# Routing, one-hot tiles and weight loads of a mixture-of-experts layer, on one core

## The chip, the cores and the metric

One core of a Trainium2 chip. The metric is the device time of one execution in microseconds (us).

## The reference, cut to what matters

```python
x = x + _L0_xattn_ref(_layernorm(x), ctx, ...)      # 16 query heads, 8 key/value heads
x = x + _L0_ffn_ref(_layernorm(x), ...)             # the part that the change touches
...                                                 # three more pairs of attention and feed-forward
def _L0_ffn_ref(x, router_logits, gating_einsum, linear, per_expert_scale, router_scale):
    ...
    probs = jax.nn.softmax(logits32, axis=-1)
    _, choices = jax.lax.approx_max_k(logits32, k=k)                # 2 of 8 experts
    ...
    sorted_xs = x_flat[xs_indices, :]                               # 4096 rows, sorted by expert
    gate_out = jax.lax.ragged_dot(sorted_xs, w_gate, group_sizes=tokens_per_expert)
    activation = jax.nn.gelu(gate_out[:, 0, :]) * gate_out[:, 1, :]
    expert_outputs = jax.lax.ragged_dot(activation, linear, group_sizes=tokens_per_expert)
    expert_outputs = expert_outputs * per_expert_scale[expert_indices, None]
    out = jnp.einsum('blkd,blk->bld', out, combine_weights)
```

There are 2048 tokens of 512 values. Every token goes to two of eight experts. Each expert has an up matrix of 512 x 1024 and a down matrix of 512 x 512.

## The kernel before, in words

The program is written by hand for each engine, and the engines meet on semaphores only. TensorE is called PE, VectorE DVE, ScalarE ACT, GpSimd POOL and SyncE SP. Layer 0's attention is the "wide" stage. `wide_steps` (line 449) yields one list of steps, and every engine goes through the same list and does its part of each step. So the order in that list is the order of the work on every engine. The expert stage follows, and its list is `block_steps` (line 1235). Between the stages stands `fence` (line 215): each of the five engines drains, adds one to a semaphore and waits until all five have done so.

The end of the wide stage forms the last rows of the layer. `late_norm` (line 386) normalises a tile of 128 rows, SP stores it to DRAM (`sp_late`, line 400), `late_ln` turns it on PE and ACT copies the high part out, and `late_low` (line 434) makes the low part on DVE. `logits` k (line 1467) multiplies 512 tokens by the router, `route` k (line 1485) turns these logits so that tokens lie on partitions, and `best` (line 1608) finds the best experts on DVE. The wide stage does routes 0 to 2 and two of the three best steps. Route 3 (first line of `pe_experts`, line 1495) and the last best step (in `dve_experts`, line 1622) lie behind the fence.

Behind the fence POOL makes small constants (line 1398 on), among them a triangle and a row of counting numbers. PE counts the tokens of each expert with matmuls, and DVE works out each token's place. A place p is block p // 128 and position p % 128. OB is a one-hot tile of the block, OS one of the position: 32 operations of 128 x 128 elements. POOL and ACT scale OB into ON, and PE multiplies OS and ON into a table that says which token stands at each place. POOL gathers the rows of a block by this table with an indirect DMA (line 1442), three blocks ahead, and scatters the results (line 1447). DVE also writes EI, three values for each of the 39 blocks: the expert, whether it differs from the one before, and which half of the weight buffers it uses. `known` tells the others that EI is there.

For a block j PE does `turn` (the gathered rows), `upper` (24 matmuls with the up weights in WU), `mid` (turns the hidden rows), `lower` (12 matmuls with the down weights in WD). Upper j + 1 is done before lower j. At blocks 3, 5, 24 and 28 a projection for the next layer is added, and at block 10 a small step. WU and WD have two halves each. SP issues `wup` and `wdown` of every block in the order of the list. It reads three registers from EI, and the issue is conditional: if the expert is the same as in the block before, nothing is moved, though the semaphore still counts. `wup` j waits until block j - 2 has used its weights, and `wdown` j until block j - 2 has used its down weights:

```python
                row = bass.ds(ex * 128, 128)
                if step == "wup":
                    sp.wait_ge(S["up"], 2 * (j - 1))
                    sp.e.dma_start(w["WU"][:, bass.ds(bu * 8192, 8192)].bitcast(F32), self.MW[row, 0:8192], cond=ch
                                   ).then_inc(S[f"moeu{j % 2}"], 16)
```

An up load is 4 MB (128 x 8192 values of 4 bytes), a down load 2 MB. In the queue of SP also stand `dca` (constants and copies for the next layer, at blocks 1, 9 and 32) and `narrow` (its weights, at block 12).

Of the kernel before, what the change touches and what calls it, by code (L numbers as in the profile page):

```python
# [17 lines left out]
NBLK = 39  # L18
# [14 lines left out]
    "ones": 1, "anym": 2, "mrow": 3, "onesb": 4, "erl": 5, "erlo": 6, "evar": 7, "oa": 8, "edl": 9, "first": 10, "eplace": 11, "eob": 12, "eoh": 13, "eone": 17, "tokens": 18, "known": 19, "eow": 20, "vdd": 21, "vzero": 22, "gqk": 23, "crl": 24, "cwl": 25, "cprob": 27, "ccc": 28,  # L33

    "ers": 1, "iota": 2, "tri": 5, "places": 7, "esel": 11, "eon1": 12, "egate": 14, "eg3": 19, "ready1": 20, "ready2": 21, "mfl": 22,
# [19 lines left out]
           "moeu0": 320, "moeu1": 304, "ht": 39, "hh_turned": 39, "up": 78, "xst": 39, "xs_turned": 39}  # L55
# [106 lines left out]
class Program:  # L162
    def __init__(self, nc, ins, out):
# [21 lines left out]
        self.rs = self.sb("rs", [128, NT], F32)  # L185
        self.st = self.sb("st", [128, NT, 6], F32)
# [262 lines left out]
    def wide_steps(self, L):  # L449
# [101 lines left out]
        if l0:  # L551
            yield "route", 2
            yield "best", 0
            yield "best", 1
# [228 lines left out]
    def sp_wide(self, sp, L):  # L783
# [4 lines left out]
        for step, g in self.wide_steps(L):  # L788
# [321 lines left out]
    def dve_wide(self, dve, L, steps=None):  # L1110
# [9 lines left out]
        for step, u in steps or self.wide_steps(L):  # L1120
# [107 lines left out]
            if step == "best":  # L1228
                self.dve_route_best(dve, u)
# [49 lines left out]
    def expert_tiles(self):  # L1279
# [26 lines left out]

        mu = self.place[0]["mu8"]
# [5 lines left out]
        stand(base + 65536, mu)  # L1313
        sb("ON", [128, 2 * NT, 2, 40], BF16)
        sb("OA", [128, NT, 8], BF16)
        sb("tri", [128, 128], BF16)
        sb("all1", [128, 128], BF16)
        sb("e8", [128, 5, 8], F32)
        sb("n8", [128, 2, 8], I32)
        sb("zero", [128, 8], F32)  # L1320
        sb("pb", [128, 2 * NT], BF16)
        stand(mu + 2048, base + 90112)
        sb("OB", [128, 2 * NT, 40], BF16)
        sb("OG", [128, 2 * NT, 3, 40], BF16)
        sb("esc", [128, 8], F32)
        sb("oh", [128, 2, NT, 8], F32)
        sb("pos", [128, NT, 8], F32)
        sb("i8f", [128, 8], F32)
        sb("jio", [128, 40], F32)
        sb("jr", [128, 40], F32)  # L1330
        sb("pf", [128, 2, NT], F32)
        sb("pi", [128, 3, 2 * NT], I32)
        sb("pl", [128, 2 * NT], F32)
        sb("g3", [128, 3, 2 * NT], BF16)
        sb("ga", [128, 2, NT], F32)
        sb("es", [128, 2, NT], F32)
        sb("number", [128, 40], F32)
        sb("tf", [1, 1], F32)

        w["OS"] = self.at("eOS", [128, 2 * NT, 128], BF16, self.xl_at + 16384)  # L1340
        stand(base + 32768, base + 65536)
# [5 lines left out]
        sb("pc", [128, 1], F32)  # L1347
        sb("trf", [128, 128], F32)
        sb("tm", [128, 2, NT, 8], F32)
        sb("te", [128, 2, NT, 8], F32)  # L1350
        sb("ge", [1, 40, 8], F32)
# [12 lines left out]
    def sp_experts(self, sp):  # L1364
# [30 lines left out]
    def pool_experts(self, pool):  # L1395
        S, w = self.S, self.W["e"]
        P1, at = S["pool_one"], ONE["esel"]
        pool.e.iota(w["i8f"][:], [[1, 8]], base=0, channel_multiplier=0, allow_small_or_imprecise_dtypes=True)
        pool.e.iota(w["jio"][:], [[1, 40]], base=0, channel_multiplier=0, allow_small_or_imprecise_dtypes=True).then_inc(P1, 1)
        pool.e.memset(w["trf"][:], 1.0).then_inc(P1, 1)  # L1400
        pool.wait_ge(P1, ONE["tri"] - 2)
        pool.e.affine_select(out=w["trf"][:], in_=w["trf"][:], compare_op=ALU.is_gt, fill=0.0, base=0,
                             pattern=[[1, 128]], channel_multiplier=-1).then_inc(P1, 1)
        pool.e.memset(w["all1"][:], 1.0)
        pool.wait_ge(P1, ONE["tri"] - 1)
        pool.copy(w["tri"][:], w["trf"][:]).then_inc(P1, 1)
        pool.e.iota(w["jr"][:], [[128, 40]], base=0, channel_multiplier=0, allow_small_or_imprecise_dtypes=True)
        pool.e.iota(w["io"][:], [[1, 128]], base=0, channel_multiplier=0, allow_small_or_imprecise_dtypes=True)
        pool.e.iota(w["ic"][:], [[1, 2 * NT]], base=0, channel_multiplier=0, allow_small_or_imprecise_dtypes=True)
# [2567 lines left out]
```

## Time and profile before

| what | value |
|---|---|
| median of 3 runs | 3536.63 us |
| lowest and highest run | 3533.78 and 3544.22 us |
| the profiled execution | 3552.24 us |
| its span, first to last instruction | 3550.5 us |
| PE busy, share of the span | 93% |
| DVE, ACT, POOL busy | 67%, 44%, 35% |
| mean granted clock of TensorE | 0.970 |

The profile is one execution. Busy shares are averages over stages that are bound by different things. The wide stage of layer 0 ends at about 794 us, the expert blocks run from about 820 to 1215 us, and two thirds of the kernel lie behind them.

### The profile page before, as it was taken

What the parts mean: (1) busy time and instruction counts of PE and PEld (TensorE: products, weight loads), DVE (VectorE), ACT (ScalarE), POOL (GpSimd) and SP (SyncE); (2) the same over time, 40 slices, a digit from 0 to 9 for tenths busy, and PEclk for the clock granted to TensorE, in tenths of its full rate; (3) what the DMA queues carried; (4) which work ended last, traced back from release to release, by engine and by line L of the source; (5) the groups of instructions that cost most, each with busy time, mean ns of one, the idle gap of its engine ahead of it and who ended that gap; (6) DMA issues with size and microseconds to landing.
All of it is one profiled execution on the core that took longest, in us unless ns stands there. A gap on an engine that the chain in (4) does not pass through costs nothing.

```text
span 3550.5 us, 60357 instructions
## 1 busy us (share of the span) xinstructions
PE 3291.5 (93%) x22499; PEld 2711.5 (76%) x22499; DVE 2377.9 (67%) x4731; ACT 1572.4 (44%) x3398; POOL 1238.5 (35%) x1169
## 2 busy tenths in 40 slices
PE   7999999997999879998999979998889999999987
PEld 6899899875777646655899855554679999999976
DVE  6677778784323368876644458776677777777786
ACT  5766666541111145553222224444245555555551
POOL 1023333342243277762322236555621111111232
PEclk9999999997999989999999999999999999999999
DMA  3356666215655210001111046563011111111101
GB/s 140 99 194 230 225 229 203 79 56 201 223 205 198 73 36 26 23 6 50 48 37 54 22 121 168 142 164 90 31 48 48 60 59 55 48 60 48 61 25 51
DMA packets 186248, 349.35 MB, mean 98 GB/s; under 512 B 20168, under 2 KB 91976, under 8 KB 181096
## 3 DMA queue, kind: packets, MB, share of 16 engines
q1 hardware_dynamic: 179720, 325.04, 28.6%
q0 software_dynamic: 6240, 20.45, 1.6%
q8 instruction: 183, 3.00, 0.4%
q14 instruction: 105, 0.86, 0.1%
HBM read 436.26 MB, written 101.97 MB: 152 GB/s over the span
## 4 chain that ended last, share of the span: by engine, by line
PE 18%; issue 14%; DVE 10%; POOL 5%; ACT 2%; DMA 2%; SPq 1%; DVEq 0%; POOLq 0%; ACTq 0%
PE banks L109 17%; POOL kst L92 2%; DMA nqT<-head_stacks 1%; POOL qst L92 1%; PE banks L222 1%; DVE K L92 1%; ACT P L83 1%; DVE qst L103 1%; SPq L106 1%; POOL nPS L92 1%; DVE P L96 1%; POOL kvl L92 1%; DVE X L92 1%; DVE st L278 1%; DVE nmx L103 1%
## 5 line engine op out<-in xcount | busy, mean ns | idle before, releaser
L92 DVE TENSOR_TENSOR X<-X,banks 128x512 f32<-128x512 f32 x352 | 238.8, 680 | 129.0 <-PE banks L109 128.7
L103 DVE TENSOR_REDUCE nmx<-banks 128x4 f32<-128x1024 f32 (+2 forms) x256 | 238.6, 953 | 122.1 <-PE banks L109 121.1
L92 POOL TENSOR_TENSOR slo<-sraw,shi 128x512 fp32r<-128x512 f32 x108 | 141.7, 1312 | 362.7 <-ACT shi L86 359.8
L83 ACT ACTIVATE nPT<-banks 128x1024 f32<-128x1024 f32 x192 | 196.2, 1023 | 143.9 <-PE banks L109 141.7
L92 POOL TENSOR_TENSOR kst<-kst,mhalf 128x4 f32<-128x4 f32 x64 | 64.6, 1010 | 558.5 <-DVE kst L97 558.5
L109 PE MATMUL banks<-XH,tT 128*128 128x256 f32 x1024 | 245.7, 284 | 7.7 <-DVE XL L92 4.5
L109 PE MATMUL banks<-XL,tT 128*128 128x256 f32 x1024 | 244.3, 283 | 0.0
L109 PE MATMUL banks<-WU,exh 128*128 (+1 forms) x624 | 209.7, 408 | 15.9 <-DMA WU<-expert_parts 14.4
L109 PE MATMUL banks<-woh,OH 128*128 128x512 f32 x512 | 214.4, 419 | 8.3 <-DVE X L92 5.4
L83 ACT ACTIVATE P<-banks,nb,qst 128x256 f32<-128x256 f32 x256 | 141.1, 561 | 180.9 <-DVE nb L92 180.9
L109 PEld LDWEIGHTS banks<-XH,tT 128*128 128x128 f32 x1024 | 197.0, 192 | 10.9 <-DVE XL L92 6.1
L109 PE MATMUL banks<-woh,OL 128*128 128x512 f32 x512 | 202.7, 396 | 0.0
L109 PE MATMUL banks<-wol,OH 128*128 128x512 f32 x512 | 202.3, 395 | 0.0
L92 POOL TENSOR_TENSOR nPS<-nPT 128x512 f32<-128x512 f32 x128 | 162.7, 1276 | 108.4 <-PE banks L109 95.8
L109 PEld LDWEIGHTS banks<-XL,tT 128*128 128x128 f32 x1024 | 196.7, 192 | 0.8
L109 PE MATMUL banks<-kvh,CX 128*128 128x256 f32 x1024 | 190.0, 283 | 0.0
L92 POOL TENSOR_TENSOR rs<-sc,mhalf 128x1 f32<-128x1 f32 x128 | 81.7, 642 | 269.7 <-DVE sc L96 269.6
L103 DVE TENSOR_REDUCE mx<-banks 128x2 f32<-128x512 f32 x256 | 174.6, 682 | 1.8 <-PE banks L109 1.5
L92 DVE TENSOR_TENSOR PL<-banks,PH 128x512 fp32r<-128x512 f32 x256 | 164.0, 681 | 14.3 <-ACT PH L86 14.1
L92 POOL TENSOR_TENSOR tHL<-thf,tHH 128x512 fp32r<-128x512 f32 x64 | 82.6, 1291 | 253.5 <-ACT tHH L86 253.5
L83 ACT ACTIVATE P<-banks,nb 128x256 f32<-128x256 f32 x256 | 117.8, 472 | 116.6 <-DVE nb L96 116.3
L96 DVE TENSOR_SCALAR P<-P,rc 128x256 f32<-128x256 f32 x512 | 164.0, 383 | 4.6
(468 smaller groups left out, 10508.9 us busy)
## 6 DMA issues: line engine op xcount, KB each, us to landing
WU<-expert_parts SPq DMA_DIRECT2D x39, 4096.0 KB
WD<-expert_parts SPq DMA_DIRECT2D x39, 2048.0 KB
CX<-context_parts SPq DMA_DIRECT2D x64, 512.0 KB, 3.3
sraw<-in_moe_w SPq DMA_DIRECT2D x96, 256.0 KB, 3.3
expert_parts<-shi SPq DMA_DIRECT2D x96, 256.0 KB
expert_parts<-slo SPq DMA_DIRECT2D x96, 256.0 KB
head_stacks<-nTK SPq DMA_DIRECT2D x48, 256.0 KB
head_stacks<-nTQ SPq DMA_DIRECT2D x48, 256.0 KB, 3.7
```

Of the source, the lines that this page charges most:

```text
L83: return self.e.activation(out, in_, func, **kw)
L92: return self.e.tensor_tensor(out, a, b, op)
L96: return self.e.tensor_scalar(out, a, s1, None, op0)
L103: return self.e.tensor_reduce(out, a, AX.X, op, **kw)
L106: return self.e.dma_start(out, in_)
L109: return self.e.matmul(out, l, r, start=start, stop=stop, skip_group_check=skip)
L222: return pe.e.transpose(out, in_, self.ident[0:n, 0:n])
L278: dve.e.bn_stats(self.st[:, t, :], self.X[:, t, :]).then_inc(S["bn"], 1)
```

## The change

The changes of order are in the two lists. Route 3 and all the finding of the best experts no longer stand behind the fence: `fence` is split into `leave` and `enter`; PE, DVE and POOL leave where they left before and enter later. POOL's constants are made in a new step `ones` of the wide stage. OS is made by two operations of 16 x 128 elements. Expert 0's up weights are loaded by SP in step `late_norm` 13, and the load of block 0 is now conditional on the first expert in use being another. SP waits, for its loads, on a value that it reads from a new table EW: for block j, twice (up) or once (down) the index of the last block before j at which the expert changed, and at least 1. The waits on `ewt` (the gates product) before the up loads are gone. The tiles of the routing lie at other addresses.

```diff
@@ def fence
+    def leave(self, e):
+        e.e.drain().then_inc(self.S["fence"], 1)
+    def enter(self, e, k):
+        e.wait_ge(self.S["fence"], 5 * k)
     def fence(self, e, k):
-        e.e.drain().then_inc(self.S["fence"], 1)
-        e.wait_ge(self.S["fence"], 5 * k)
+        self.leave(e)
+        self.enter(e, k)
@@ def wide_steps
         yield "late_low", 11
-        for t in (14, 15):
-            yield "late_ln", t
         if l0:
+            yield "ones", 0
             yield "route", 0
+        yield "late_ln", 14
+        if l0:
             yield "route", 1
+        yield "late_ln", 15
         for t in (12, 13, 14, 15):
             yield "late_low", t
...
         if l0:
             yield "route", 2
-            yield "best", 0
-            yield "best", 1
@@ def sp_wide
                 self.sp_late(sp, g)
+            if l0 and step == "late_norm" and g == 13:
+                sp.wait_ge(S["y"], 128)
+                sp.dma(self.W["e"]["WU"][:, 0:8192].bitcast(F32), self.MW[0:128, 0:8192]).then_inc(S["moeu0"], 16)
@@ def pool_wide
+            if step == "ones":
+                self.pool_route_ones(pool)
@@ def dve_wide
-            if step == "best":
-                self.dve_route_best(dve, u)
@@ def block_steps
-        for j in range(3):
-            yield "wup", j
-            if j < 2:
-                yield "wdown", j
+        yield "wup", 0
+        yield "wdown", 0
+        yield "wup", 1
+        yield "wup", 2
+        yield "wdown", 1
@@ def sp_experts
                     bu, ch = 0, None
+                    if step == "wup":
+                        ch = sp.e.value_load(w["one"][0:1, 1:2], min_val=0, max_val=1)
+                        sp.wait_ge(S["moeu0"], 16)
                 else:
                     sp.wait_ge(S["dve_one"], ONE["known"])
-                    sp.wait_ge(S["pe_one"], ONE["ewt"])
+                    if step == "wdown":
+                        sp.wait_ge(S["pe_one"], ONE["ewt"])
...
                 if step == "wup":
-                    sp.wait_ge(S["up"], 2 * (j - 1))
+                    if j > 1:
+                        free = sp.e.value_load(w["EW"][0:1, 0, j:j + 1], min_val=1, max_val=2 * NBLK)
+                        sp.wait_ge(S[f"moeu{j % 2}"], 16 * (j // 2 + 1 - j % 2))
+                        sp.e.wait_ge(S["up"], free)
...
                 else:
-                    sp.wait_ge(S["down"], j - 1)
+                    if j > 1:
+                        free = sp.e.value_load(w["EW"][0:1, 1, j:j + 1], min_val=1, max_val=NBLK)
+                        sp.wait_ge(S[f"x{j % 2}"], 16 * (j // 2 + 1))
+                        sp.e.wait_ge(S["down"], free)
@@ def pool_experts (the constants moved, unchanged, to pool_route_ones, behind sp "ov" 64)
+        self.enter(pool, 1)
         pool.wait_ge(S["dve_one"], ONE["tokens"])
@@ def pe_experts
         for i in range(2 * NT):
-            pe.wait_ge(S["dve_one"], ONE["eoh"] + i // 8)
+            pe.wait_ge(S["dve_one"], ONE["eoh"] + i // NT)
...
+        self.enter(pe, 1)
         for step, j in self.block_steps():
...
-                pe.wait_ge(S[f"moeu{j % 2}"], 16 * (j // 2 + 1))
+                pe.wait_ge(S[f"moeu{j % 2}"], 16 * (j // 2 + 2 - j % 2))
@@ def dve_experts
-        self.dve_route_best(dve, 2)
         dve.e.memset(w["zero"][:], 0.0)
+        for k in range(3):
+            self.dve_route_best(dve, k)
...
+        dve.ts(w["one"][0:1, 1:2], w["tf"][0:1, 0:1], 1.0, None, ALU.min)
         dve.copy(w["one"][0:1, 0:1], w["tf"][0:1, 0:1]).then_inc(S["dve_one"], 1)
...
-        dve.copy(pb[:], pi[:, 2, :]).then_inc(S["dve_one"], 1)
-        dve.wait_ge(S["rt"], a)
-        c = rt(dve.copy(w["pl"][:], pi[:, 1, :]))
+        dve.copy(pb[:], pi[:, 1:3, :]).then_inc(S["dve_one"], 1)
         dve.wait_ge(S["dve_one"], ONE["eplace"])
+        dve.wait_ge(S["fence"], 5)
...
-        for i in range(2 * NT):
-            m = dve.ts(w["OS"][:, i, :], w["iob"][:], w["pl"][:, i:i + 1], None, ALU.is_equal)
-            if i % 8 == 7:
-                m.then_inc(S["dve_one"], 1)
+        for k in range(2):
+            place = pb[:, 0, NT * k:NT * k + NT].unsqueeze(2).to_broadcast([128, NT, 128])
+            dve.tt(w["OS"][:, NT * k:NT * k + NT, :], w["iob"][:].unsqueeze(1).to_broadcast([128, NT, 128]), place, ALU.is_equal
+                   ).then_inc(S["dve_one"], 1)
...
         rt(dve.copy(EI[:, 2, :], r0(2)))
+        b = rt(dve.tt(r0(3), r0(1), w["jio"][0:1, :], ALU.mult))
+        dve.wait_ge(S["rt"], b)
+        b = rt(dve.e.tensor_tensor_scan(r0(4), r0(3), r0(7), 0.0, ALU.max, ALU.add))
+        dve.wait_ge(S["rt"], b)
+        for k in range(2):
+            rt(dve.ts(w["EW"][:, k, 1:40], r0(4)[:, 0:39], 2.0 - k, 1.0, ALU.mult, ALU.max))
@@ def pe_program, dve_program, pool_program
-        self.fence(pe, 1)
+        self.leave(pe)
...
```

## Rows read from the trace of the kernel before

**Rows 1.** Waits of PE, 820 to 1216 us: us in total, times, longest

```profile
PE banks L109 <- DMA WU<-expert_parts: 14.4, 8, 3.6
```

**Rows 2.** Timeline of PE, turning hidden rows: start, us, engine, line, operation

```profile
832.85 0.60 PE L222 MATMUL banks<-ident,eh 128*128 128x128 f32 x4
...
843.71 0.60 PE L222 MATMUL banks<-ident,eh 128*128 128x128 f32 x4
...
1066.83 0.60 PE L222 MATMUL banks<-ident,eh 128*128 128x128 f32 x4
...
1075.98 0.60 PE L222 MATMUL banks<-ident,eh 128*128 128x128 f32 x4
...
1086.85 0.60 PE L222 MATMUL banks<-ident,eh 128*128 128x128 f32 x4
...
1200.49 0.60 PE L222 MATMUL banks<-ident,eh 128*128 128x128 f32 x4
```

**Rows 3.** Timeline of PE, first up matmul of blocks 5 and 13 [idle before]

```profile
876.39 0.79 PE L109 MATMUL banks<-WU,exh 128*128 x1 [2.89 <-DMA WU<-expert_parts]
...
959.71 0.50 PE L109 MATMUL banks<-WU,exh 128*128 x1 [1.01 <-DMA WU<-expert_parts]
```

**Rows 4.** Timeline of SP's issues, 834 to 947 us

```profile
834.70 0.11 SPq L1383 DMA_DIRECT2D WU<-expert_parts  x1
836.86 0.09 SPq L1387 DMA_DIRECT2D WD<-expert_parts  x1
...
859.87 0.37 SPq L1383 DMA_DIRECT2D WU<-expert_parts  x1
...
946.15 0.36 SPq L1383 DMA_DIRECT2D WU<-expert_parts  x1
```

**Rows 5.** Timeline of PE, 782 to 822 us

```profile
782.78 0.66 PE L222 MATMUL banks<-ident,late 128*128 128x128 f32 x4 [1.00 <-DVE XL L92]
...
784.42 1.95 PE L109 MATMUL banks<-e,elgT 16*128 16x8 f32 x16
...
794.13 1.87 PE L109 MATMUL banks<-e,elgT 16*128 16x8 f32 x8 [1.42 <-DVEq L217]
...
811.65 0.71 PE L109 MATMUL banks<-eON,eOS 128*128 128x80 bf16 x8 [0.59 <-DVE eOS L96]
820.13 1.12 PE L222 MATMUL banks<-ident,exs 128*128 128x128 f32 x4 [7.77 <-DMA exs<-rows_in,etok]
```

**Rows 6.** Timeline of DVE, 796 to 812 us

```profile
796.11 0.19 DVE L89 COPY eLG<-banks 128x32 f32<-128x32 f32 x1 [2.08 <-PE banks L109]
...
797.23 0.16 DVE L1620 FIND_INDEX8 ei<-em,eLG 128x8 uint32<-128x8 f32 x1
...
802.77 1.49 DVE L92 TENSOR_TENSOR eOB<-ejb,epb 128x1280 bf16<-128x1280 bf16 x1
804.18 7.41 DVE L96 TENSOR_SCALAR eOS<-eiob,epl 128x128 bf16<-128x128 bf16 x32
```

**Rows 7.** Timeline of POOL, 804 to 815 us

```profile
804.34 2.33 POOL L92 TENSOR_TENSOR eON<-eOB,eicb 128x1280 bf16<-128x1280 bf16 x1 [3.75 <-DVE eOB L92]
...
813.58 1.28 POOL L1442 DMA_INDIRECT exs<-rows_in,etok  x1 [0.86 <-DVE etok L1715]
```

**Rows 8.** Instructions on tile eOS: duration ns min/median/max, first and last start

```profile
L96 DVE TENSOR_SCALAR eOS<-eiob,epl x32: 240/241/2374, 804.2 to 811.4; 128x128 bf16<-128x128 bf16 x32
```

**Rows 9.** Timeline of all engines, 637 to 643 us, POOL and DVE

```profile
637.77 1.21 DVE L92 TENSOR_TENSOR wql<-wqr,wqh 128x1024 fp32r<-128x1024 f32 x1
...
638.19 4.15 POOL L92 TENSOR_TENSOR slo<-slo,sraw 128x512 f32<-128x512 f32 x2 [1.63 <-DMA sraw<-in_L_ffn_factors]
...
638.90 2.32 DVE L92 TENSOR_TENSOR wol<-wor,woh 128x1024 fp32r<-128x1024 f32 x1
```

**Rows 10.** Line L1442, the gather issued at 813.58, and the one at 821.53

```profile
DMA to landing us min/median/max: 6.5/6.5/6.5
...
DMA to landing us min/median/max: 3.3/3.3/3.3
```

More of the change, by code:

```diff
@@ L31 @@
     "elt": 4, "etot": 5, "ecount": 6, "etab": 7, "ewt": 8, "vdp": 9, "tsum": 10, "clt": 11, "cgate": 12,
-    "ones": 1, "anym": 2, "mrow": 3, "onesb": 4, "erl": 5, "erlo": 6, "evar": 7, "oa": 8, "edl": 9, "first": 10, "eplace": 11, "eob": 12, "eoh": 13, "eone": 17, "tokens": 18, "known": 19, "eow": 20, "vdd": 21, "vzero": 22, "gqk": 23, "crl": 24, "cwl": 25, "cprob": 27, "ccc": 28,
-    "ers": 1, "iota": 2, "tri": 5, "places": 7, "esel": 11, "eon1": 12, "egate": 14, "eg3": 19, "ready1": 20, "ready2": 21, "mfl": 22,
+    "ones": 1, "anym": 2, "mrow": 3, "onesb": 4, "erl": 5, "erlo": 6, "evar": 7, "oa": 8, "edl": 9, "first": 10, "eplace": 11, "eob": 12, "eoh": 13, "eone": 15, "tokens": 16, "known": 17, "eow": 18, "vdd": 19, "vzero": 20, "gqk": 21, "crl": 22, "cwl": 23, "cprob": 25, "ccc": 26,
+    "iota": 1, "tri": 4, "places": 6, "ers": 7, "esel": 11, "eon1": 12, "egate": 14, "eg3": 19, "ready1": 20, "ready2": 21, "mfl": 22,
     "mask": 16, "rl_in": 48, "n_wd": 64, "n_pos": 80, "mbias": 96, "gqk_in": 128, "cw": 144,
@@ L185, in __init__ @@
         self.rs = self.sb("rs", [128, NT], F32)
+        self.st_at = self.top
         self.st = self.sb("st", [128, NT, 6], F32)
@@ L1305, in expert_tiles @@
         w["end"] = place[0]
+        w["EW"] = self.at("eEW", [1, 2, 40], I32, self.st_at)
         mu = self.place[0]["mu8"]
@@ L1311, in expert_tiles @@
         sb("i8", [128, NT, 8], U32)
-        stand(base + 65536, mu)
-        sb("ON", [128, 2 * NT, 2, 40], BF16)
+        sb("zero", [128, 8], F32)
+        stand(base + 65536 + 2048, mu)
+        sb("oh", [128, 2, NT, 8], F32)
         sb("OA", [128, NT, 8], BF16)
-        sb("tri", [128, 128], BF16)
-        sb("all1", [128, 128], BF16)
+        sb("pos", [128, NT, 8], F32)
+        sb("tm", [128, 2, NT, 8], F32)
         sb("e8", [128, 5, 8], F32)
         sb("n8", [128, 2, 8], I32)
-        sb("zero", [128, 8], F32)
-        sb("pb", [128, 2 * NT], BF16)
+        sb("pb", [128, 2, 2 * NT], BF16)
+        sb("pf", [128, 2, NT], F32)
+        sb("pi", [128, 3, 2 * NT], I32)
+        sb("tf", [1, 1], F32)
         stand(mu + 2048, base + 90112)
         sb("OB", [128, 2 * NT, 40], BF16)
+        sb("ON", [128, 2 * NT, 2, 40], BF16)
         sb("OG", [128, 2 * NT, 3, 40], BF16)
         sb("esc", [128, 8], F32)
[L1326 to L1336, printed above, removed]
         sb("number", [128, 40], F32)
-        sb("tf", [1, 1], F32)
         w["OS"] = self.at("eOS", [128, 2 * NT, 128], BF16, self.xl_at + 16384)
-        stand(base + 32768, base + 65536)
+        stand(self.place[0]["QH"], self.place[0]["P"])
         sb("io", [128, 128], F32)
@@ L1347, in expert_tiles @@
         sb("pc", [128, 1], F32)
+        sb("i8f", [128, 8], F32)
+        sb("jio", [128, 40], F32)
+        sb("jr", [128, 40], F32)
         sb("trf", [128, 128], F32)
-        sb("tm", [128, 2, NT, 8], F32)
+        sb("tri", [128, 128], BF16)
+        sb("all1", [128, 128], BF16)
         sb("te", [128, 2, NT, 8], F32)
+        sb("es", [128, 2, NT], F32)
+        sb("ga", [128, 2, NT], F32)
+        sb("g3", [128, 3, 2 * NT], BF16)
         sb("ge", [1, 40, 8], F32)
@@ L1397, in pool_experts @@
         P1, at = S["pool_one"], ONE["esel"]
[L1398 to L1409, printed above, removed]
-        pool.e.iota(w["pc"][:], [[1, 1]], base=1, channel_multiplier=1, allow_small_or_imprecise_dtypes=True).then_inc(P1, 1)
-        pool.wait_ge(P1, ONE["places"] - 1)
-        pool.copy(w["iob"][:], w["io"][:])
-        pool.copy(w["jb"][:], w["jio"][:])
-        pool.copy(w["icb"][:], w["ic"][:]).then_inc(P1, 1)
         te, es, ga, sm = w["te"], w["es"], w["ga"], w["sm"]
@@ L1454, in pool_experts, with pool_route_ones @@
                 self.pool_key_rows(pool, *j[:2])
+    def pool_route_ones(self, pool):
+        S, w, P1 = self.S, self.W["e"], self.S["pool_one"]
+        pool.wait_ge(S["ov"], 64)
+        pool.e.iota(w["i8f"][:], [[1, 8]], base=0, channel_multiplier=0, allow_small_or_imprecise_dtypes=True)
+        pool.e.iota(w["jio"][:], [[1, 40]], base=0, channel_multiplier=0, allow_small_or_imprecise_dtypes=True).then_inc(P1, 1)
+        pool.e.memset(w["trf"][:], 1.0).then_inc(P1, 1)
+        pool.wait_ge(P1, ONE["tri"] - 2)
+        pool.e.affine_select(out=w["trf"][:], in_=w["trf"][:], compare_op=ALU.is_gt, fill=0.0, base=0,
+                             pattern=[[1, 128]], channel_multiplier=-1).then_inc(P1, 1)
+        pool.e.memset(w["all1"][:], 1.0)
+        pool.wait_ge(P1, ONE["tri"] - 1)
+        pool.copy(w["tri"][:], w["trf"][:]).then_inc(P1, 1)
+        pool.e.iota(w["jr"][:], [[128, 40]], base=0, channel_multiplier=0, allow_small_or_imprecise_dtypes=True)
+        pool.e.iota(w["io"][:], [[1, 128]], base=0, channel_multiplier=0, allow_small_or_imprecise_dtypes=True)
+        pool.e.iota(w["ic"][:], [[1, 2 * NT]], base=0, channel_multiplier=0, allow_small_or_imprecise_dtypes=True)
+        pool.e.iota(w["pc"][:], [[1, 1]], base=1, channel_multiplier=1, allow_small_or_imprecise_dtypes=True).then_inc(P1, 1)
+        pool.wait_ge(P1, ONE["places"] - 1)
+        pool.copy(w["iob"][:], w["io"][:])
+        pool.copy(w["jb"][:], w["jio"][:])
+        pool.copy(w["icb"][:], w["ic"][:]).then_inc(P1, 1)
     def pool_gate_parts(self, pool):
@@ L1680, in dve_experts @@
         dve.wait_ge(S["rt"], a)
[L1681 to L1683 removed]
+        rt(dve.e.tensor_scalar(pi[:, 1, :], pi[:, 0, :], 127, None, ALU.bitwise_and))
+        a = rt(dve.e.tensor_scalar(pi[:, 2, :], pi[:, 0, :], 7, None, ALU.arith_shift_right))
+        dve.wait_ge(S["rt"], a)
         dve.wait_ge(S["pool_one"], ONE["places"])
[L1685 to L1687 removed]
+        dve.copy(pb[:], pi[:, 1:3, :]).then_inc(S["dve_one"], 1)
         dve.wait_ge(S["dve_one"], ONE["eplace"])
+        dve.wait_ge(S["fence"], 5)
         for i in range(2):
@@ L3839, in dve_program @@
         self.dve_wide(dve, 0)
-        self.fence(dve, 1)
+        self.leave(dve)
         self.dve_experts(dve)
@@ L3862, in pool_program @@
         self.pool_wide(pool, 0)
-        self.fence(pool, 1)
+        self.leave(pool)
         self.pool_experts(pool)
```

8 lines of the change are left out of this document (2 added, 6 removed).

## Prediction

> **What bounds the kernel now.** The change touches one stretch: the routing of layer 0 and the 39 expert blocks behind it. I read the waits of TensorE (PE) there first. Its largest entry is PE waiting for expert up weights, 14.4 us in 8 waits [rows 1]. A wait is not a price, so next comes the pace of the blocks in PE's timeline, by the four transposes of the hidden rows that each block has once. Two neighbours without any event are 9.15 us apart; with one extra key or value projection between them 10.87, so that costs 1.72; from block 0 to block 37 it is 367.64 us [rows 2]. 37 plain intervals are 338.6, the four projections 6.9, a small extra step at block 10 0.2. So 22.0 us are lost to the eight waits: more than the 14.4 idle, because matmuls behind a long stall run slow: 0.79 us for the first behind 2.89 us of idle, 0.50 behind 1.01 [rows 3]. One wait is at block 1. The interval before it ends (832.85 to 843.71) is 10.86, so 1.7 is lost there [rows 2]. The other seven, at the first block of each new expert (5, 9, 13, 18, 23, 28, 31), share 20.2.
>
> Why they come is in SyncE's (SP's) queue. An issue that moves data takes 0.35 to 0.38 us there, a skipped one 0.08 to 0.11. The load for block 5 goes out at 859.87 and PE starts on it at 876.39, 16.5 us later; the quickest, for block 13, takes 13.6 (946.15 to 959.71) [rows 3, 4]. SP may issue only when block j-2 has used its weights, about a block and a half ahead of need; that is shorter than the load.
>
> Ahead of the blocks nothing overlaps. PE's third quarter of routing is followed by 1.42 us for the barrier and 1.87 for the fourth [rows 5]; DVE finds the best experts from 796.11, builds OB at 802.77 and 32 one-hot tiles from 804.18 in 7.41 us [rows 6]; PE's last eight matmuls on them take 0.71 [rows 5]; POOL issues the first gather at 813.58 [rows 7], and PE turns its rows at 820.13 after 7.77 idle [rows 5]. This is one chain, and every us on it is a us of the kernel.
>
> **The change, part by part.**
>
> *Order and barrier.* PE idles 1.00 us before the turn of row tile 14, the two early routes behind it take 1.95 for 16 matmuls, 0.98 each [rows 5]. Route 0 now lies in the idle time, route 1 before turn 15, which logits 3 alone needs. Logits 2 starts at 782.78 + 0.6 (turn) + 0.98 + 0.6 = 784.95 instead of 786.3: 1.35 us. Route 2 then ends near 791.4 in place of 792.7, and route 3 follows without the 1.42. DVE no longer leaves the barrier between quarters: its 1.3 us for quarter 2 (the length of the same work from 796.11 to 797.3 [rows 6]) end at 792.7, when the fourth can begin, not at 796.11. That is 3.4. An added minimum and the place of the wider cast cost 0.1 each, the zero fill of 0.07 leaves the chain: **3.2 us**. Bounds: if the slower matmuls return (1.87 for route 3) and the 1.35 is lost, 1.5; if the logits matmuls behind them, about half of which ran slow, keep their pace too, 4.7 (an estimate). POOL's constants move into a stretch in which it only waits for DVE; their first reader comes some 10 us later, so they cost nothing, and 10 us late they would cost what they cost now.
>
> *Two operations for the one-hot tiles.* Before, 32 operations of 0.24 us that overlap, one of which took 2.37 [rows 8]: POOL's ON (804.34, 2.33 us [rows 7]) ran just then. Elsewhere two DVE operations with two SBUF inputs show the same exclusion both ways: POOL's subtraction of 638.19 starts when wql ends, and wol then takes 2.32 in place of 1.21 [rows 9]. The new operations have the operand form of OB, one side repeated and one broadcast: 1.49 us for 1280 elements [rows 6]; wql has 1.21 for 1024 [rows 9]. That is 1.1 ns an element, so 2048 take 2.3. The first starts at the end of OB, POOL's ON waits behind it, takes 2.3, and the second follows; less two overlaps of 0.1 that is 6.7 us in place of 7.4, of which the last operation's own overlap gives 0.1 back. PE's tail is now 16 matmuls, 1.4 us in place of 0.71. Net **0.1 us** less. Bounds: without exclusion 2.2 less; if POOL has to wait for both, all 32 matmuls come behind, 1.4 more. On this the Trainium skill, VectorE: DVE Perf Modes, section "The perf-mode tier table", has 1224 ns for a two-tensor operation of 2048 bf16 elements. By it each operation would be 1.1 us shorter and this part would bring 2.2. The row for 1280 elements has no such rate, and the sum goes by the row.
>
> *Expert 0's up weights early.* SP issues 4 MB behind row tile 13's store, at about 779.5, once the last output product is done. By the slowest block load (16.5) they are in at 796. SP then waits for them, skips the normal load (if the first expert is 0; with eight experts in use it is), and loads the 2 MB of down weights at about 800.5. Before, the first gather was issued while 6 MB were moving and needed 6.5 us; a later one in a quiet stretch 3.3 [rows 10]. Its first issue is 0.3 us longer than later ones, so 3.6: **2.9 us**. Bounds 0 and 3.2. Row tiles 14 and 15 are stored behind the 4 MB; OB waits for them at 799.6, which is 3 us later than the load's latest end.
>
> *Block 1.* SP no longer waits for the gates product before wup 1 and issues it some 12 us ahead of need: **1.7 us**, bounds 0 and 1.7.
>
> *Register waits.* DVE computes them in four operations, 0.7 us, behind the tokens that POOL needs: they delay only `known`, which PE wants 14 us later. On SP a step is 2.16 us (834.70 to 836.86 [rows 4]); a fourth register adds about a third of three reads, 0.6, so 2.8 a step, 5.5 a block, under 9.15. Behind the waiting SP instruction are the skipped loads, the constants of the next stage and the next real load. The register holds the start of the previous expert, so wup(c) may go when its buffer is free, but wup(c+1) waits until block c-1 is through upper, and wdown(c+1) until block c-1 is through lower. For the next change c2 = c+4 the load is therefore issued at least 3 steps (8.1 us) behind the lower step of c-1 and needed three blocks and a turn, 27.8 us, behind it: 19.7 us ahead against 13.6 to 16.5. For c+3 (28 to 31) 15.9 plus the projection's 1.7; for 9 to 13 another 3.8 us of SP's copies lie between: 15.9. The narrowest is block 5: the floor of 1 holds wdown 2 until block 0's down product is done, just before block 1's transposes (843.71 [rows 2], less the 7.9 us won by then: 835.8). Then wup 4, wdown 3, seven constant loads (an estimate: 0.5 each, from the 0.35 of a plain issue) and wup 5 follow, 847.7. It is needed at 876.39 - 2.89 - 7.9 = 865.6 [rows 3], 17.9 later. All seven losses go: **20.2 us**. Bounds 14 (block 5 keeps its 5.9) and 20.2. What is late next is nothing on PE: blocks at 9.15.
>
> **Sum**: 3.2 + 0.1 + 2.9 + 1.7 + 20.2 = 28.1 us. The profiled execution has 3552.24 us (span 3550.5), so it would be 3524.1; it lies 15.6 above the median of the runs, and nothing in the sum scales with that, so 3536.63 - 28.1 = **3508.5 us**.
>
> **Rivals.**
> *First boundary stays.* SP's steps are longer than 2.8, or wup 5 goes with the constants just issued and takes over 17.9 us. Block 5 keeps up to 5.9: 3514.4. For: the 16.5 of this very load. Chance 0.2.
> *The routing gain is given back.* The late row tiles land behind the 4 MB (on each DMA engine descriptors are taken in ring order: the Trainium skill, DMA: Bandwidth & Descriptors, "Queues, rings and completion order"; no row here shows it), or the slow level comes back: the 3.2 go and OB waits some us more. 3511.7 to 3514. Chance 0.15.
> *The stalls change their place.* Loads of 6 MB beside gathers and scatters (a gather needs up to 6.5 beside them [rows 10]) or some other queue hold PE at the boundaries; half of the 20.2 and the gather's 2.9 stay: 3521.5. If all 20.2 stay, the change does not do what it says: 3528.7. Chance 0.12.
> *Slower.* SP becomes the pace. If a register read or a wait on a register costs far more than the reads in this trace, a step passes 4.6 us and two of them the block's 9.15. At 5.4 us a step 37 blocks lose 1.65 each, 61 us, against 28: 3569. It decides from 4.6 on and outweighs the gain from about 5.0. Against it: 2.16 with three reads [rows 4]. Chance 0.03.
>
> **How the numbers follow.** The forecast has 0.5. Its own range by the bounds: 3505 to 3513. Eight in ten with the first two rivals, half of the third and some us of run to run spread: 3502 to 3522. A measurement of this kernel tells about 0.3% (10.6 us) from no change. Faster by more needs 3526 or less: all but the last tenth, 0.93; within it 0.04; slower 0.03.
>
> **What would show it.** In the profile of after: transposes of block 0 and 37 about 345.7 us apart (338.6 + 7.1); no wait for WU at changes of expert, real up loads 20 to 45 us ahead of use; first gather landing in under 4 us; the fourth quarter's best experts from about 792.7; OS in two operations near 2.3 us, one of them near 4.4 with POOL's ON inside. Wrong would be: a wait for WU at block 5, SP steps over 4.6 us, OB waiting for a DMA, or a distance from block 0 to 37 that stays over 360.

## The result, and the profile of the changed kernel

The changed kernel takes 3519.5 us (median of 6 runs, 3518.7 to 3526.61) against 3544.33 for the kernel before on the same chip (6 runs, 3533.78 to 3551.73): ratio 0.9938, 95% interval [0.9918, 0.9958], or 22 us less by the ratio, between 15 and 29; the two medians lie 24.8 apart. The forecast was 28.1 less and 3508.5 us, 3505 to 3513 by the bounds of its terms and 3502 to 3522 with rivals and spread. The direction holds, and so does the wider range; the time lies outside the narrower one, and the gain was forecast too large. Of the 11.0 us between 3508.5 and 3519.5, 7.7 are in the base: three more runs moved the median of before from 3536.63 to 3544.33. The profiled execution of the changed kernel has 3518.88 us (span 3517.1), against the 3524.1 that the prediction gave for it from the profile of before.

The two profiles, set side by side by stages, with those of three more executions from later runs of the same two kernels (each stage is the distance between the first starts of the events named, in us; the ends are good to 0.1):

| stage | before | before, 2nd | after | after, 2nd | after, 3rd |
|---|---|---|---|---|---|
| start to store of row tile 13 | 778.9 | 782.3 | 778.9 | 783.0 | 783.4 |
| to the cast of the best experts | 18.51 | 16.12 | 13.30 | 14.86 | 13.28 |
| to the turn of block 0 | 22.72 | 22.57 | 20.37 | 20.76 | 20.57 |
| to block 0's hidden rows | 12.71 | 12.57 | 11.75 | 12.98 | 13.13 |
| block 0 to block 37 | 367.64 | 365.77 | 347.12 | 347.14 | 347.15 |
| from there to the end | 2349.9 | 2344.7 | 2345.7 | 2340.2 | 2347.3 |

Two stages that the change does not touch, the first and the last, differ by up to 4.5 and 9.7 us between executions. The first pair of profiles is therefore 33.4 us apart although the kernels differ by 22.

First the waits of PE in after from 820 to 1184 us, which is the expert stretch. These are all that come to over 1 us, where before had 14.4 us for WU [rows 1]:

```profile
PE banks L109 <- DVE ehl L92: 2.2, 1, 2.2
PE banks L109 <- issue: 1.2, 1, 1.2
```

PE's timeline of after, for [rows 5] and the ends of [rows 2] (start, us, engine, line, operation, idle before):

```profile
781.70 1.05 PE L109 MATMUL banks<-e,elgT 16*128 16x8 f32 x8
782.77 0.66 PE L231 MATMUL banks<-ident,late 128*128 128x128 f32 x4
783.36 1.05 PE L109 MATMUL banks<-e,elgT 16*128 16x8 f32 x8
784.35 0.66 PE L231 MATMUL banks<-ident,late 128*128 128x128 f32 x4
...
788.62 2.21 PE L109 MATMUL banks<-e,elgT 16*128 16x8 f32 x16
...
805.80 1.25 PE L109 MATMUL banks<-eON,eOS 128*128 128x80 bf16 x16 [0.88 <-DVE eOS L92]
812.57 1.08 PE L231 MATMUL banks<-ident,exs 128*128 128x128 f32 x4 [5.53 <-DMA exs<-rows_in,etok]
...
823.87 0.61 PE L231 MATMUL banks<-ident,exs 128*128 128x128 f32 x4
824.32 0.60 PE L231 MATMUL banks<-ident,eh 128*128 128x128 f32 x4
826.11 0.50 PE L109 MATMUL banks<-WU,exh 128*128 x1 [1.19 <-issue]
...
834.92 0.60 PE L231 MATMUL banks<-ident,eh 128*128 128x128 f32 x4
...
864.08 0.60 PE L231 MATMUL banks<-ident,eh 128*128 128x128 f32 x4
...
873.23 0.60 PE L231 MATMUL banks<-ident,eh 128*128 128x128 f32 x4
...
1171.44 0.60 PE L231 MATMUL banks<-ident,eh 128*128 128x128 f32 x4
```

Route 0 stands ahead of the turn of row tile 14, route 1 between the turns of 14 and 15, and routes 2 and 3 are one group of 16 with no barrier between. From block 4 to block 5 (864.08 to 873.23) it is 9.15 us, the plain interval: the first boundary has gone. From block 0 to block 1 it is still 10.60 (824.32 to 834.92), where 9.15 was forecast.

DVE's timeline of after, for [rows 6]:

```profile
792.20 0.19 DVE L89 CAST esm<-ei 128x32 f32<-128x32 uint32 x1
...
797.67 1.49 DVE L92 TENSOR_TENSOR eOB<-ejb,epb 128x1280 bf16<-128x1280 bf16 x1
799.08 6.66 DVE L92 TENSOR_TENSOR eOS<-eiob,epb 128x2048 bf16<-128x2048 bf16 x2
...
807.77 0.18 DVE L1746 TENSOR_SCALAR etok<-etok 128x40 int32<-128x40 int32 x1
```

POOL's timeline of after, for [rows 7]:

```profile
797.66 1.60 POOL L92 TENSOR_TENSOR ees<-ete 128x32 f32<-128x32 f32 x1
799.24 4.36 POOL L92 TENSOR_TENSOR eON<-eOB,eicb 128x1280 bf16<-128x1280 bf16 x1
...
808.83 1.24 POOL L1450 DMA_INDIRECT exs<-rows_in,etok  x1 [1.96 <-issue]
```

SP's issues in after, for [rows 4]:

```profile
779.27 0.43 SPq L106 DMA_DIRECT2D WU<-expert_parts  x1
...
835.44 0.08 SPq L1412 DMA_DIRECT2D WD<-expert_parts  x1
838.20 0.08 SPq L1405 DMA_DIRECT2D WU<-expert_parts  x1
...
847.93 0.36 SPq L1405 DMA_DIRECT2D WU<-expert_parts  x1
```

The pair of OS operations takes 6.66 us (forecast 6.7), an SP step 2.76 (835.44 to 838.20; forecast 2.8), and block 5's up load goes out at 847.93 (forecast 847.7), where it went at 859.87 [rows 4]. PE's timeline of after shows it starting on it at 864.43, with no idle time:

```profile
863.85 0.39 PE L109 MATMUL banks<-WD,ehh 128*128 x1
...
864.43 0.48 PE L109 MATMUL banks<-WU,exh 128*128 x1
```

That is 16.5 us behind the issue, as long as this load took before, and not the 17.9 of the forecast. In the two later profiles of after it is 16.9 and 16.7, also without a loss. The gather goes from 808.83 to PE's turn at 812.57 in 3.74 us, against 6.55 before [rows 5, 7].

### The profile page after: what moved, and what is told of

Read it like the earlier page. It is cut to its first block, busy times and chain, and to the rows that moved or that the text cites. A ratio compares the mean times of both kernels' runs of the same rounds, so it can differ in the third digit from the quotient of the medians.

```text
span 3517.1 us, 60631 instructions
## 1 busy us (share of the span) xinstructions
PE 3274.5 (93%) x22499; PEld 2700.7 (77%) x22499; DVE 2377.7 (68%) x4705; ACT 1573.2 (45%) x3398; POOL 1242.3 (35%) x1169
## 4 chain that ended last, share of the span: by engine, by line
PE 17%; issue 15%; DVE 10%; POOL 5%; ACT 2%; DMA 2%; SPq 1%; DVEq 0%; POOLq 0%; ACTq 0%
PE banks L109 16%; POOL kst L92 2%; DMA nqT<-head_stacks 1%; POOL qst L92 1%; DVE K L92 1%; ACT P L83 1%; DVE qst L103 1%; PE banks L231 1%; SPq L106 1%; POOL nPS L92 1%; DVE P L96 1%; DVE X L92 1%; POOL kvl L92 1%; DVE st L287 1%; DVE PL L92 1%
```

## The experiments

The theory under test was the prediction's own: seven boundaries are the bulk, the routing and the gather bring some 3 us each, the one-hot pair next to nothing. The rival was that the gain between the profiles comes from how the executions differ: TensorE's level in the logits, and stages that nobody touched.

**The two kernels once more.** No edit; the kernel before ran as a kernel of its own beside its usual runs.

> The kernel before once more, for its profile: how far two profiles of one kernel differ, and where. Theory A: its routing and its expert blocks repeat within 0.5 us (block 0 to block 37 in 367.6 us, the eight waits for up weights 14.4 us), and what differs between runs (its runs go from 3533.8 to 3551.7) lies in stages that the change does not touch. Rival B: the waits for weights themselves vary by some us from run to run, and so does the distance from block 0 to block 37.

> The changed kernel once more, beside the kernel before on one chip. Theory A: the whole gain lies between the end of the wide stage and the end of the expert blocks, 29.0 us in the two profiles (block 37's transposes of the hidden rows at 1200.49 before and 1171.44 after), and nothing behind it changes; then the timed difference is 27 to 31 us (ratio 0.991 to 0.9925), and from block 37 to the end the span is as long as before within the spread of repeated runs. Rival B: the stages behind the experts give part of it back; then the timed difference is 18 to 23 us here too (ratio 0.9935 to 0.995), and the rest behind block 37 is some 5 us longer than in the kernel before.

> The changed kernel a third time, timed. Like with like (each kernel's profile with slow logits, each without) the profiles give 24.5 to 25.8 us from row tile 13's store to the end of the blocks. Theory: that is the gain, ratio 0.9927 to 0.9931, and the two lower results so far (0.9938, 0.9947) are spread. Rival: some 5 us are given back in a part that the profiles do not show; the ratio is 0.994 or more a third time.

Before against itself, 12 runs: 3542.25, ratio 1.0008 [0.9995, 1.0022]. After: 3520.93, ratio 0.9947 [0.9931, 0.9963]; on another chip 3519.63, ratio 0.9931 [0.9911, 0.995]. With the first result the mean of the three is 0.9939, 21.7 us less. The table above has their stages. The waits for weights are not one number either. In before's second profile, from 820 to 1216 us as in [rows 1], they are

```profile
PE banks L109 <- DMA WU<-expert_parts: 12.5, 8, 3.4
```

where the first had 14.4, and block 0 to 37 is 1.9 us shorter. So the second theory of that run (the stalls themselves vary) is the right one, beside the first (untouched stages vary). For the changed kernel, after_again came out at 19 us less by its ratio, as its rival had it, but not by that rival's cause: its last stage is not longer. The third run's 0.9931 is what its theory said.

In the logits, matmuls that take 0.40 us at a granted clock of 1.00 (the 2.4 GHz level; after, 784.8 to 788.5) took about 0.63 in some executions, where it was 0.50 (the 1.2 GHz level; before, 787.1 to 790.0): 7 of 32 in before's first profile, 8 in after's second, none in the other three. That comes with the run, not with the kernel. Like with like, the routing stage goes from 18.51 to 14.86 (3.65 less) with the slow ones, and from 16.12 to 13.30 (2.82) without.

**Constants in place of the registers.**

```diff
-                        free = sp.e.value_load(w["EW"][0:1, 0, j:j + 1], min_val=1, max_val=2 * NBLK)
-                        sp.e.wait_ge(S["up"], free)
+                        sp.wait_ge(S["up"], 2 * (j - 1))
...
-                        free = sp.e.value_load(w["EW"][0:1, 1, j:j + 1], min_val=1, max_val=NBLK)
-                        sp.e.wait_ge(S["down"], free)
+                        sp.wait_ge(S["down"], j - 1)
```

> The changed kernel with the loads' waits put back to constants (up for block j-2 done, down for block j-2 done), and without the reads of their registers; all else as changed. Theory A (the constant wait is what made the loads late): the seven waits for up weights at the first blocks of new experts are back, block 0 to block 37 takes 347.1 + 20.2 = 367.3 us, the time is 20 us more than the changed kernel's. Rival (the loads are late because of traffic around them or of the gates wait, and the early order alone cures it): block 0 to 37 stays under 355 us, at most 8 us more.

3537.38, ratio 0.9984 [0.9972, 0.9995]: of the gain 5.7 us are left. Block 0 to 37 is back at 364.64 (367.64 and 365.77 in before). The largest of PE's waits in its expert stretch:

```profile
PE banks L109 <- DMA WU<-expert_parts: 12.7, 7, 3.6
```

PE's timeline of the same kernel, around the first boundary:

```profile
867.03 0.60 PE L231 MATMUL banks<-ident,eh 128*128 128x128 f32 x4
870.92 0.79 PE L109 MATMUL banks<-WU,exh 128*128 x1 [3.29 <-DMA WU<-expert_parts]
881.12 0.60 PE L231 MATMUL banks<-ident,eh 128*128 128x128 f32 x4
```

Seven waits, one for each change of expert, and block 5 costs 14.09 in place of 9.15. In this kernel the load left at 853.96 and was needed at 867.6. The register waits are shown to be the cause: 17.5 us in the profile (364.64 less 347.14), 16.5 in the medians (3537.38 less 3520.93), 13 by the two ratios (0.9984 and 0.9947). The 20 that was expected from the first profile did not come back.

**The registers alone.** The kernel before, with the table EW and the waits on it, and nothing else of the change.

```diff
@@ before, sp_experts
+                    if j > 1:
+                        free = sp.e.value_load(w["EW"][0:1, 0, j:j + 1], min_val=1, max_val=2 * NBLK)
+                        sp.wait_ge(S[f"moeu{j % 2}"], 16 * (j // 2))
+                        sp.e.wait_ge(S["up"], free)
-                    sp.wait_ge(S["up"], 2 * (j - 1))
... (the same for "down", and the four operations for EW on DVE)
```

> The kernel before with the register waits alone: the table EW and the waits of the up and down loads on it; order, barrier, one-hot tiles, the load of block 0 and the gates wait as before. Theory: the seven waits at new experts go, block 0 to block 37 takes 367.64 - 20.2 = 347.4 us (like the two profiles of the kernel before, 17 to 20 less), up to block 0 nothing changes; 18 to 20 us less than the kernel before, ratio 0.9943 to 0.995. Rival: without the other parts (the gates wait moved away, the early load) SP starts too late and the wait at block 5 stays: 353 us, 14 us less.

3528.51 (7 runs), ratio 0.9957 [0.9939, 0.9974], 15 us less, where 18 to 20 were expected; block 0 to 37 is 348.88, between the theory's 347.4 and the rival's 353. Six boundaries are plain, that of block 5 is not, as PE's timeline of this kernel shows:

```profile
874.75 0.60 PE L223 MATMUL banks<-ident,eh 128*128 128x128 f32 x4
876.55 0.49 PE L109 MATMUL banks<-WU,exh 128*128 x1 [1.20 <-DMA WU<-expert_parts]
885.36 0.60 PE L223 MATMUL banks<-ident,eh 128*128 128x128 f32 x4
```

10.61 us. The load for block 5 goes out at 859.99, 25.3 us behind block 0's hidden rows (834.69); in after it is 23.6 (824.32 to 847.93). PE wants it 15.4 us later and gets it after 16.6. Here the up loads still wait for the gates product, so SP starts its steps at 836.54 and is behind with them when block 0's down weights come free: wdown 2 goes 1.37 us behind block 1's hidden rows (845.55 to 846.92), in after 0.52 (834.92 to 835.44). Of the 1.7 us between 25.3 and 23.6 that is half (0.85); 0.26 are the longer block 1 (10.86 against 10.60), and the steps behind are 0.6 slower. So 1.5 us of the seven boundaries' gain come only with the rest of the change. By this timeline it is the gates wait, which the prediction priced at block 1 only; no run takes that wait away alone, and the order of `wup` 2 and `wdown` 1 changed with it. After has next to no margin at block 5: in the kernel with the barrier below, the same load goes out 17.1 us ahead of PE's start on it (852.21 to 869.29), and that interval still is 9.47 us.

**No early load.** Expert 0's up weights are loaded behind the barrier again.

```diff
-            if l0 and step == "late_norm" and g == 13:
-                sp.wait_ge(S["y"], 128)
-                sp.dma(self.W["e"]["WU"][:, 0:8192].bitcast(F32), self.MW[0:128, 0:8192]).then_inc(S["moeu0"], 16)
```

> The changed kernel without the early load of expert 0's up weights: block 0 loads them when the first expert is known, as before. Theory A: the first gather again shares the DMA engines with 6 MB and lands 6.5 us after its issue instead of 3.7, all else as changed; 2.8 us more, and the scale values (4 KB) land 2.5 us after their issue instead of 6. Rival: the early load was worth nothing or cost time, since it held those values and POOL's work on them back; then the time is the same or up to 2 us less.

3524.95, ratio 0.9949 [0.9936, 0.9963]. The times cannot tell it from after (3520.93). The profile can: gather to turn takes 6.19 us against 3.67 to 3.84 in the three profiles of after, and the stage to the turn of block 0 is 23.02 against 20.37 to 20.76. POOL's timeline of this kernel, the first gather:

```profile
808.52 1.24 POOL L1444 DMA_INDIRECT exs<-rows_in,etok  x1 [1.97 <-issue]
```

And PE's, the turn of its rows:

```profile
814.71 1.08 PE L231 MATMUL banks<-ident,exs 128*128 128x128 f32 x4 [7.98 <-DMA exs<-rows_in,etok]
```

**32 one-hot operations.** The changed kernel with the old OS, released in two halves as in the new.

```diff
+        for i in range(2 * NT):
+            m = dve.ts(w["OS"][:, i, :], w["iob"][:], w["pl"][:, i:i + 1], None, ALU.is_equal)
+            if i % NT == NT - 1:
+                m.then_inc(S["dve_one"], 1)
```

> The changed kernel with the 32 small one-hot operations back, their results released in two halves as now. Theory: one of the 32 waits for POOL's operation as before, they take 7.4 us in all against 6.66, and the first gather goes 0.7 us later. Rival (the two operations gain what they save in fixed cost, 2.9 us): the 32 take 2.9 us more than the two.

One run, 3520.05. OS takes 7.42 us where the pair takes 6.66, and the gather goes out 11.92 us behind the start of OB against 11.16. Before, it was 10.81 (802.77 to 813.58) [rows 6, 7]. So the two operations bring 0.76, and something else takes 1.1 back. Half of it is the release in two halves: from the end of OS to DVE's first operation on PE's table it was 0.81 us (811.59 to 812.40) and is 1.34 here (806.40 to 807.74). The other half, 0.56, is a later start of the gather behind the finished table, of which more below.

**Route order; barrier.** Two one-run kernels. The first turns row tiles 14 and 15 ahead of routes 0 and 1, as before; in the second PE passes the barrier ahead of route 3.

```diff
@@ first
+        for t in (14, 15):
+            yield "late_ln", t
         yield "route", 0
-        yield "late_ln", 14
         yield "route", 1
-        yield "late_ln", 15
@@ second, ahead of route 3 on PE
+        self.enter(pe, 1)
```

> The changed kernel with the turns of row tiles 14 and 15 ahead of routes 0 and 1, as before. Theory: the 1.0 and 0.4 us of idle time of PE are back, logits 2 starts at 1.4 us later behind the store of row tile 13, and if TensorE's granted clock falls in the logits as it did in the kernel before, the best experts come 3 us later in all; from row 13's store to the cast of the best experts 14.7 to 16.4 us instead of 13.3. Rival: order is worth nothing, since DVE's own work on the first 8 tiles sets the end: 13.3 to 13.6.

> The changed kernel with PE entering the next stage ahead of route 3, so behind all five engines. Theory: the price of the barrier was DVE's finding of the best experts inside it; since DVE now leaves before it begins with that, the barrier opens when PE itself has drained, and this costs 0.1 to 0.8 us. Rival: the barrier itself costs the 1.4 us that PE waited, and the best experts come 1.4 us later.

The times, 3530.07 and 3523.86 in one run each, tell nothing here: runs of one kernel lie further apart than that. To the cast of the best experts the first has 14.75 us, the second 13.48, after 13.28 and 13.30, all without slow logits. The order is worth 1.45; the barrier by itself costs 0.2, as route 3 in PE's timeline of the second shows:

```profile
793.83 1.05 PE L109 MATMUL banks<-e,elgT 16*128 16x8 f32 x8 [0.31 <-POOLq L218]
```

Around block 5 of the same kernel, SP's issue of the up load, then PE's rows:

```profile
852.21 0.36 SPq L1405 DMA_DIRECT2D WU<-expert_parts  x1
...
868.64 0.60 PE L231 MATMUL banks<-ident,eh 128*128 128x128 f32 x4
869.29 0.49 PE L109 MATMUL banks<-WU,exh 128*128 x1
...
878.11 0.60 PE L231 MATMUL banks<-ident,eh 128*128 128x128 f32 x4
```

The 1.42 us before route 3 [rows 5] were thus not the barrier's own price: PE waited there for DVE, which reached it only after the best experts of the third quarter, whose last operation starts at 793.87. Moving these behind it is what removed the rest.

**A version with the two leftovers taken out.** The turn of block 1 stands ahead of the gates product, and DVE makes the second half of ON itself, ahead of OS.

```diff
@@ block_steps
+        yield "turn", 1
+        yield "rows", 4
         yield "gates", 0
-        yield "turn", 1
-        yield "rows", 4
@@ dve_experts, behind OB (POOL's own operation is gone)
+        dve.tt(w["ON"][:, :, 1, :], w["OB"][:], w["icb"][:].unsqueeze(2).to_broadcast([128, 2 * NT, 40]), ALU.mult
+               ).then_inc(S["pool_one"], 1)
```

> The changed kernel with two further edits. First, the turn of block 1's rows is put ahead of the gates product on PE. Theory: the wait of 1.2 us at block 1 is the chain turn, ACT copy, DVE subtraction that was hidden under the wait for the weights before; the gates product (1.85 us) then hides it, block 0 to block 1 takes 9.2 to 9.5 us instead of 10.6. Rival: the loads of block 1 arrive only then; the distance stays 10.6. Second, the second half of ON is made by DVE (1.4 us) instead of POOL (2.3 us, which keeps DVE from its second one-hot operation). Theory: DVE and POOL exclude each other for whole operations with two SBUF inputs; without POOL's operation the pair of OS takes 4.5 us instead of 6.66, and OB to the end of OS 7.5 instead of 8.1. Rival: the pair is slow by itself and stays at 6.6 us; then this edit costs 1.4 us. Both edits together: 1.5 to 2 us less than the changed kernel, under what the timed runs can tell.

> The version with block 1's turn ahead of the gates product and ON made by DVE, once more, on the same chip as the changed kernel. Its profile showed 1.43 us less at block 1 and 0.6 less from OB to the end of OS. Theory: 2 us less than the changed kernel, so a ratio 0.0006 under it. Rival: it is 5 us or more under it, as the first two sets of runs had it (0.9924 against 0.9947 on another chip).

3516.32, ratio 0.9924 [0.9905, 0.9943], and 3518.65, ratio 0.9934 [0.9914, 0.9955], the second beside after at 0.9931 on the same chip. DVE's timeline of the first of the two runs:

```profile
802.12 1.49 DVE L92 TENSOR_TENSOR eOB<-ejb,epb 128x1280 bf16<-128x1280 bf16 x1
803.71 1.49 DVE L92 TENSOR_TENSOR eON<-eOB,eicb 128x1280 bf16<-128x1280 bf16 x1
805.12 4.48 DVE L92 TENSOR_TENSOR eOS<-eiob,epb 128x2048 bf16<-128x2048 bf16 x2
```

PE's timeline of the same run, hidden rows of blocks 0 and 1:

```profile
828.12 0.61 PE L231 MATMUL banks<-ident,eh 128*128 128x128 f32 x4
837.27 0.60 PE L231 MATMUL banks<-ident,eh 128*128 128x128 f32 x4
```

Without POOL's ON beside it the pair takes 4.48 us, 2.2 less; DVE pays 1.5 of that for ON, so from the start of OB to the end of OS it is 7.48 against 8.07. Block 0 to 1 is 9.15, and block 0 to 37 345.7, the very figure of the prediction. By the profile this version has 2.0 us less than after (0.6 and 1.4); the timings cannot tell the two apart.

## Why the prediction was right, and where it was not

Most of the mechanisms were right; the sum was not. The step that failed first is the pricing: the term for the seven boundaries was read off one profile of stalls that vary, 20.2 us where three measurements have 18.7 in the mean. The second is the path at block 1, taken to be free behind the wait for weights. The third is the base: "3536.63 - 28.1" rests on three runs, and six have 3544.33. That 3519.5 lies within 3502 to 3522 is owed to the allowance for rivals and spread; no rival came true as a whole.

**Register waits: the mechanism as forecast, the size too large.** Forecast 20.2 us for seven boundaries. All seven go. What they cost before is not one number: 20.2 in the first profile, 18.3 in the second of before (365.77 less 345.7 and less 1.74 for block 1), 17.5 with the constants. Mean 18.7. The prediction took the one profile that it had, an execution at 3552.24, above all six runs timed beside the result, and said that nothing in the sum scales with that. That step failed: the sum was made of stalls, and the stalls were at their dearest there. Between the two profiles of before it is mostly block 9 (an interval of 13.32 us in the first, 10.60 in the second); block 5 has 15.08 and 14.99 in them, and 14.09 with the constants.

**Block 1: the step that failed outright.** Forecast 1.7, measured 0.26 (10.86 to 10.60). The wait for WU went, but "what is late next is nothing on PE" was wrong here. PE turns block 1's rows at 823.87, just ahead of block 0's hidden rows, and block 1's up product must wait until ACT and DVE have split them: the 1.19 us of idle in front of 826.11 in the timeline of after. The profile names no releaser for it, but ACT's and DVE's timelines of after have the chain, whose last link ends at 825.91:

```profile
824.52 0.60 ACT L86 ACTIVATE exh<-banks 128x512 fp32r<-128x512 f32 x1 [4.29 <-PE banks L231]
825.22 0.69 DVE L92 TENSOR_TENSOR exl<-banks,exh 128x512 fp32r<-128x512 f32 x1 [0.49 <-ACT exh L86]
```

In before this chain lay hidden under the load. The turn ahead of gates gives the plain 9.15, which shows it.

**Order and barrier: right.** Forecast 3.2; 3.65 and 2.82 between executions at the same level of the clock, of which the order has 1.45 (forecast 1.35). The forecast's upper bound, 4.7, and the 5.2 between the first two profiles both have the slower logits in them.

**One-hot in two operations: the pair as forecast, the later gather unseen.** Forecast 0.1 less, measured 0.35 more (10.81 to 11.16, OB to gather). Foreseen: the exclusion, and the pair at 6.7. The Trainium skill, VectorE: DVE Perf Modes, section "The perf-mode tier table", gives 1224 ns for a two-tensor operation of 2048 bf16 elements; with POOL out of the way the pair here took 4.48 us for two, so the trace does not agree for these repeated and broadcast operands. PE's last half takes 1.25 us instead of 0.71, which is close to forecast (1.4). Not foreseen: POOL starts the gather 0.88 us behind the token table (807.77 + 0.18 to 808.83), before only 0.32 (813.08 + 0.18 in its timeline to 813.58). This 0.56 is in every kernel built on the change, and in none of the three executions of kernels that keep before's order. Its cause is open. What the record has: for POOL's idle time in front of the gather the profile names DVE's table in before (0.86 us) and no releaser in the changed kernels, where the gather starts 1.96 to 1.97 us behind POOL's last product in all ten executions. The barrier's wait (`enter`) now stands in POOL's program between that product and the gather; no run moves it.

**Early load: right.** Forecast 2.9; 2.8 from gather to turn between before and after, and 2.45 against the kernel without it (6.19 less 3.74), 2.3 to 2.65 by the stage. Some 0.4 of the 2.8 thus came with other parts of the change.

**Sum.** By the profiles 3.2 - 0.35 + 2.8 + 0.3 + 18.7 = 24.65 us; the stages of the table between the store of row tile 13 and block 37 give 25.2 (means 419.3 and 394.1). The timed ratios give 21.7. 25.2 would be a ratio of 0.9929, inside the intervals of 0.9938 and 0.9931 and just outside that of 0.9947. Where those last 3 us stay, the runs do not settle in full, but a stage behind block 37 is unlikely. Over all kept profiles the last stage takes 2347.8 us in the mean of the three executions with before's order and 2346.6 in the mean of the ten with the new one (2340.2 to 2353.2), and the first stage 780.1 and 780.5. Neither has grown by 3 us, so chance in the timed runs is the likelier part. Of the 28.1, 3.4 are terms that were mis-sized (the boundaries 1.5, block 1 1.4, the one-hot tiles with the gather's start 0.45), and the rest is that.

**Rivals.** The first boundary did not stay: block 5 is plain in after; 1.5 of its 5.9 us stay where the gates wait is kept. But it was nearer than the 0.2 that it had been given: 17.9 us were forecast for a load that takes 16.5, and 16.5 is what it got; in the kernel with the barrier the interval is 0.3 us longer. The stalls did not change their place: in the blocks of after PE waits for no DMA by more than 1 us in total. The routing gain was not given back, though the slow level did return in one of the three profiles of after (14.86 us to the cast against 13.3). The scale values of the experts, a load of 4 KB issued at 789.96 behind the 4 MB, did land only at 795.9 (6 us, before 2.5), and POOL waited for them, but OB did not. The Trainium skill, DMA: Bandwidth & Descriptors, section "Queues, rings and completion order", has it that each DMA engine takes its descriptors in ring order; the row agrees, for 795.9 is also when the 4 MB of 779.27 were due (an estimate, from the 16.5 us of block 5's load). SP's step is 2.76, far from 4.6.

## What to carry to other kernels

A wait for a buffer that is often kept (experts that do not change from block to block) can be moved back to the last real use by a value worked out on the chip; it costs 0.6 us a step here, and takes seven stalls away. Price a stall by the interval between two equal events, not by its idle time, and over more than one execution; then ask of each wait removed which other chain it covered. When many small operations become two, look at what was released in pieces before.

## What the runs showed of the hardware that was not expected

- The level of TensorE's clock in the logits is not a property of the kernel: 7 to 11 of 32 matmuls at about 0.63 us instead of 0.40 in four of the thirteen executions, none in others of the same code.
- The exclusion of DVE and POOL catches small operations too. POOL's `ees`, 128 x 32 elements, takes 1.60 us beside OB, and 0.24 to 0.28 where it runs ahead of it.
- A wait on a register value is cheap here: SP's step grows from 2.16 to 2.76 us with the read and the wait on it together. How the 0.6 splits between them is not shown.
- A load of 4 KB took 5.9 us with 4 MB ahead of it, and 2.5 without.
